# A graph layer on one core: node biases moved from bf16 products into the weights, one of four node rows normalised by ScalarE

## The chip, the cores and the metric

The kernel runs on one core of one Trainium2 chip. The metric is the device time of one execution in microseconds (us); lower is better. The engines are named as in the profile: PE is TensorE (PEld its weight loads), DVE is VectorE, ACT is ScalarE, POOL is GpSimd, SP is SyncE, which only issues transfers here. PSUM is the memory that PE writes its sums into, eight banks of 128 x 512 float32.

## The reference, cut to what matters

50,000 nodes of 256 features, 12,500 edges sorted by target `dst`.

```
h   = x @ Wn.T + bn                        # first layer: attention over the edges
a   = softmax over the edges of one dst of leaky_relu(((h[src] + edge_attr @ We.T + be) * attn).sum(-1))
x1  = layernorm(x + relu(segment_sum(h[src] * a, dst)))
                                           # second layer: dst and src change roles
mean = segment_sum(x1[dst], src) / max(count, 1)
out = layernorm(x1 + x1 @ W1.T + b1 + mean @ W2.T + b2)
```

`layernorm` takes mean and variance over the 256 features, without scale or shift. Most nodes have no edge, so for most of them `mean` is zero and `relu(...)` adds nothing.

## The kernel before

The work runs in five stages.

1. Setup: weights are loaded and turned, the edges' keys are split in digits, one-hot rows of the keys are made by DVE and ACT, and `biases` (L903 and on) writes each bias as three bf16 rows that add up to it. The identity is added into `w1T`, so that `x1 @ W1.T + x1` is one product.
2. Two counting sorts of the edges (`sort` on PE, `tiles` on DVE), by `dst` and by `src`. Beside the end of the second, POOL gathers the rows `x[src]` of 100 edge tiles, and DVE takes their dot products with the attention vector (L750 on tile `X`, `s_xdot`).
3. `by_dst`: 25 groups of four edge tiles; the first layer's aggregate is added to the nodes' rows in DRAM (`z_scratch`).
4. `dense`: 98 groups g of 512 nodes (128 partitions x 4 rows, the last one smaller). This is the stage that the change edits most.
5. `by_src`: 25 groups of edge tiles. The neighbours' mean is built, the node's own row is gathered again, both are multiplied, and the result is scattered over `out_rows`.

In `dense` each engine walks its own list in program order; only semaphores tie them together. One step of the loop, called body g here:

- PE: product of group g, first half p=0 (two rows of the four: for each row one bf16 product of `ones16` with `bias16`, L1243, then the float32 products with `w1T`, L1246); then both halves of the turn (transposes, L1236) of group g+1; then product half p=1 of group g.
- DVE: reciprocal of the deviation of x rows g+2; statistics (L915) of product half p=0 of g; normalises the four x rows of g+2 (L747); statistics of product half p=1 of g; statistics of the raw x rows g+3 (two instructions); reciprocal (L985) and `nmr` = -mean/deviation (L750) for the output of g.
- ACT: square root (L559) of the product's variance of g; square root of the x variance of g+3; then, when `nmr` is there, copies (L555) of the turned group g+2 from PSUM to `xT` and the output rows of g (L564), two at a time.

So a group's x rows are measured in one body, normalised in the next, turned in the one after it and multiplied one later. PSUM banks 0 and 1 hold turned rows, banks 4 to 7 the products, by parity of g.

In `by_src` (body q) POOL gathers own rows of q (four transfers), waits until they have landed, and scatters the output of q-3 (four transfers). PE does four aggregate tiles with a turn after each and then products with `w2T` and `w1T`, also with a bias product ahead of each row.

The functions the diff touches follow.

Of the kernel before, what the change touches and what calls it, by code (L numbers as in the profile page):

```python
# [25 lines left out]
HOOK = 48  # L26

# [25 lines left out]
def build(nc, x, src, dst, edge_attr, Wn, bn, We, be, attn, W1, b1, W2, b2, out):  # L53
# [24 lines left out]
    with ExitStack() as ctx:  # L78
# [41 lines left out]
        bias16 = sb("bias16", [P, 2, D], BF16)  # L120
# [40 lines left out]
        bias32 = agg[0][0:3, :, 0:D]  # L161
        bias_rest = agg[1][0:3, 0:2, 0:D]
# [22 lines left out]
        nmr = sb("nmr", [P, 4, GT])  # L185
        eps_c = sb("eps_c", [P, 1])

# [52 lines left out]
        s_x1 = sem("x1_ready")  # L240
# [5 lines left out]
        s_nm2 = sem("r_scales")  # L246
# [34 lines left out]
        s_enm = sem("edge_r_scales")  # L281
# [5 lines left out]
        s_rc = sems("reciprocals", 6)  # L287
# [134 lines left out]
        def _(pool):  # L422
# [90 lines left out]
            for h in range((T - sent[0]) // 2):  # L513
                pool.wait_ge(s_x1, GT * h + GT)
                order_src(2)
# [4 lines left out]
            for t in range(T):  # L520
                pool.wait_ge(s_x1, GT * (HOOK + 8 + (G - HOOK - 14) * t // T))
                wait(pool, s_nb[t % 4], 16 * (t // 4))
                gather(X[:, t, 0:D], z_dram, column(idx_dst[SRC], t), s_nb[t % 4])
# [24 lines left out]
        def _(act):  # L548
            a = nc.scalar

            def turned_copy(dst_i, src_bank, ready, n_ready, users, copied):
                act.wait_ge(ready, n_ready)
                for s, n in users:
                    wait(act, s, n)
                a.copy(xT[dst_i][:].rearrange("p a b c -> p (a b c)"), src_bank[:, :]).then_inc(copied, 1)  # L555
# [20 lines left out]
            for i, b in enumerate((bn, b1, b2)):  # L576
                act.dma_start(bias32[:, i, :], b.partition_broadcast(3)).then_inc(s_small, 16)
# [50 lines left out]
            def dense_copy(h, h_par, p):  # L628
                turned_copy(2 * h_par + p, bank[p], s_tp, 2 * h + p + 1, [(s_r, 2 * (h - 2) + p + 1)], s_tpc)
# [49 lines left out]

            root(0, s_st1, 1, s_sq1)  # L680
            root(1, s_st1, 2, s_sq1)
            for p in range(2):
                dense_copy(0, 0, p)
# [7 lines left out]
            def dense(g, m, u):  # L691
# [3 lines left out]
                act.wait_ge(s_nm2, g + 1)  # L695
# [12 lines left out]
            def by_src(q, m, u):  # L708
                def cp(p, node):
                    if in_range(q, 1, Q + 1):  # L710
                        h = q - 1
                        ready, done = (s_tc, s_tcc) if node else (s_tb[SRC], s_tbc[SRC])
                        turned_copy(2 * node + p, bank[node], ready, 2 * h + p + 1,
                                    [(s_er, 2 * (h - 1) + p + 1)], done)
# [10 lines left out]
                if in_range(q, 2, Q + 2):  # L725
                    hu = (u - 2) % 4
                    act.wait_ge(s_enm, q - 1)
# [8 lines left out]
        def _(dve):  # L736
# [166 lines left out]
            def biases():  # L903

                then(v.tensor_tensor(bias32[:, 1, :], bias32[:, 1, :], bias32[:, 2, :], ALU.add))
                rest = bias32[:, 0:2, :]
# [4 lines left out]
                v.tensor_copy(bias16[0:3], rest).then_inc(s_bias, 1)  # L911

# [19 lines left out]
            def scales(slot, rows):  # L932
                return stt(nmr[0:rows, slot, :], stats[0:rows, slot, :, 1], -1.0, rstd[0:rows, slot, :], ALU.mult, ALU.mult)

            def normalise(buf, slot, rows, ready):
                for j in range(GT):
# [25 lines left out]
            def third_stats():  # L962
                dve.wait_ge(s_x1, GT)
                first_stats(2)

            def dense(g, m, u):
# [4 lines left out]
                turns = counted(m, u, 0, 2) + 1  # L971
# [77 lines left out]
            biases()  # L1049
# [7 lines left out]

            for t in range(T):
# [57 lines left out]
            n_m = [G // 2 + (i % 2 < G % 2) for i in range(4)]  # L1116

            def by_src(q, m, u):
# [15 lines left out]
                if in_range(q, 2, Q + 2):  # L1134
                    dve.wait_ge(s_esq, q - 1)
                    invert(2 + u % 2, P, n_m[2 + u % 2] + counted(m, u, -2, 2) + 1)
                    scales(2 + u % 2, P).then_inc(s_enm, 1)
# [6 lines left out]
        def _(pe):  # L1144
# [94 lines left out]
            def products(o, terms, bias, n=P):  # L1239

                for jj in range(2):
                    to = o[0:n, jj * D:(jj + 1) * D]
                    mm(to, ones16[:, 0:n], bias16[:, bias, :], start=True, stop=False)  # L1243
                    for i, (buf, w) in enumerate(terms):
                        for c in range(2):
                            ins = mm(to, buf[:, jj, c, 0:n], w[:, c, :], start=False,  # L1246
# [4 lines left out]
            def turn(h, hu, p):  # L1251
                pe.wait_ge(s_x1, GT * h + 2 * p + 2)
# [3 lines left out]
            def product(h, par, p):  # L1256
                pe.wait_ge(s_tpc, 2 * h + p + 1)
                wait(pe, s_y, GT * (h - 2) + 2 * p + 2)
                products(rbank(par, p), [(xT[2 * par + p], w1T)], 1, parts(h)).then_inc(s_r, 1)
# [4 lines left out]

            pe.wait_ge(s_xdot, T)
# [37 lines left out]
            def by_dst(q, m, u):  # L1303
# [10 lines left out]
                def prod_b(p):  # L1314
                    if in_range(q, 1, Q + 1):
# [3 lines left out]
                        products(rbank(par, p), [(xT[2 * par + p], wnT)], 0).then_inc(s_h, 1)  # L1319
# [28 lines left out]
            def by_src(q, m, u):  # L1348
# [14 lines left out]
                if in_range(q, 1, Q + 1):  # L1363
                    h = q - 1
                    for p in range(2):
# [5 lines left out]
                        products(rbank((u - 1) % 2, p), [(xT[p], w2T), (xT[2 + p], w1T)], 1).then_inc(s_er, 1)  # L1371
# [22 lines left out]
```

## Time and profile before

| what | value |
|---|---|
| median of 3 runs | 1460.25 us (1457.04 to 1461.46) |
| profiled execution: its own time, span | 1457.04 us, 1457.1 us |
| PE busy | 1242.0 us, 85% |
| DVE busy | 1092.5 us, 75% |
| ACT busy | 784.9 us, 54% |
| POOL busy | 750.0 us, 51% |
| chain that ended last | PE 59%, DMA 9%, POOL 9%, issue 8%, ACT 7%, DVE 6% |

A busy share is an average over all five stages and says little on any one of them. In the chain of waits a stretch is put down to the engine that the end of the kernel was waiting for at that moment. PE instructions overlap: one matmul row shows a start and a duration that includes the drain, so what a matmul costs PE is the distance from one start to the next, and the chain of waits shows that distance.

### The profile page before, as it was taken

The numbers are of one execution on the slowest core, as the hardware profiler recorded it, in microseconds if no ns is written. First come the engines' busy times: TensorE is split into PE (matmuls) and PEld (weight loads), VectorE is DVE, ScalarE is ACT, GpSimd is POOL, SyncE is SP. The second block draws the span as 40 slices with busy tenths as digits, with TensorE's granted clock in tenths as the row PEclk, the third lists the DMA queues.
The fourth block names the chain that finished last, engine by engine and source line by source line (L and its number), as shares of the span: only waits on it lengthen the run. The fifth ranks groups of instructions, "written<-read, shape, count | busy, mean of one in ns | idle before, by whom it ended". The sixth has DMA issues, their size and how long they took to land.

```text
span 1457.1 us, 26741 instructions
## 1 busy us (share of the span) xinstructions
PE 1242.0 (85%) x7210; PEld 1047.6 (72%) x7210; DVE 1092.5 (75%) x3970; ACT 784.9 (54%) x1768; POOL 750.0 (51%) x731
## 2 busy tenths in 40 slices
PE   4499867960199999679999999999998999999994
PEld 3388756850088888568888888888886888778783
DVE  8888876885555555278888888888898787867761
ACT  5655773630044444347777777777764444444542
POOL 1057762677767777733433103555531555655563
PEclk9899998985599999889999999999999999999997
DMA  6889898989256666556666767898872233223221
GB/s 201 261 199 216 182 288 227 311 264 370 72 80 91 100 94 91 66 178 229 218 217 225 221 222 255 291 300 293 306 244 90 90 99 91 86 88 96 85 79 42
DMA packets 118161, 260.71 MB, mean 179 GB/s; under 512 B 23505, under 2 KB 56872, under 8 KB 118084
## 3 DMA queue, kind: packets, MB, share of 16 engines
q1 hardware_dynamic: 75738, 193.82, 42.4%
q0 software_dynamic: 40128, 64.45, 19.6%
q10 hardware_dynamic: 2218, 1.58, 0.3%
q8 instruction: 28, 0.46, 0.1%
q14 instruction: 49, 0.40, 0.1%
HBM read 182.23 MB, written 130.49 MB: 215 GB/s over the span
## 4 chain that ended last, share of the span: by engine, by line
PE 59%; DMA 9%; POOL 9%; issue 8%; ACT 7%; DVE 6%; ACTq 0%; POOLq 0%; DVEq 0%
PE bank L1246 32%; PE bank L1236 8%; PE bank L1224 5%; PE bank L1291 4%; DMA xin<-z_scratch,idx_src 4%; PE bank L1287 4%; PE bank L1243 4%; POOL out_rows L465 4%; POOL xin L462 3%; ACT aggn L602 3%; DMA X<-in_x,idx_src 2%; DVE X L747 2%; PE bank L1175 2%; DMA yout<-low_digits_scratch 2%; ACT sel L650 1%
## 5 line engine op out<-in xcount | busy, mean ns | idle before, releaser
L1246 PE MATMUL bank<-w1T,xT 128*128 128x256 f32 x1968 | 491.2, 380 | 0.0
L1246 PEld LDWEIGHTS bank<-w1T,xT 128*128 128x128 f32 x1968 | 343.4, 190 | 66.4 <-issue 0.3
L471 POOL DMA_INDIRECT order_scratch<-pay,rank_i x200 | 196.0, 980 | 240.8 <-DVE xin L747 105.9
L564 ACT ACTIVATE yout<-bank,nmr,rstd 128x256 f32<-128x256 f32 x492 | 251.7, 577 | 7.3 <-DVE nmr L750 7.3
L555 ACT COPY xT<-bank 128x512 f32<-128x512 f32 x346 | 203.0, 588 | 37.6 <-PE bank L1236 25.0
L915 DVE BATCH_NORM_STATS2 stats<-xin 128x6 f32<-128x512 f32 x246 | 158.8, 687 | 76.0 <-DMA xin<-z_scratch,idx_src 54.6
L915 DVE BATCH_NORM_STATS2 stats<-bank 128x6 f32<-128x512 f32 x246 | 168.5, 694 | 58.7 <-PE bank L1246 58.1
L663 ACT COPY agg<-bank 128x257 f32<-128x257 f32 (+1 forms) x200 | 74.4, 372 | 223.3 <-PE bank L1291 216.4
L510 POOL DMA_INDIRECT z_scratch<-xin,idx_out x100 | 156.4, 1564 | 53.3 <-ACT xin L676 30.1
L747 DVE TENSOR_SCALAR xin<-xin,stats,rstd 128x256 f32<-128x256 f32 x492 | 172.2, 412 | 1.0
L465 POOL DMA_INDIRECT out_rows<-yout,idx_out x100 | 100.0, 1000 | 140.6 <-DMA xin<-z_scratch,idx_src 71.8
L462 POOL DMA_INDIRECT X<-z_scratch,idx_dst x100 | 94.9, 949 | 141.7 <-DVE xin L747 112.5
L559 ACT ACTIVATE std<-stats,eps_c 128x4 f32<-128x4 f32 x271 | 81.0, 300 | 151.4 <-DVE stats L915 143.1
L1243 PE MATMUL bank<-bias,ones 128*128 128x256 bf16 (+1 forms) x592 | 161.5, 273 | 0.7 <-ACT yout L564 0.4
L1224 PE MATMUL bank<-sel,agg 128*128 128x196 f32 x800 | 155.8, 339 | 0.0
L1236 PE MATMUL bank<-ident,xin 128*128 128x128 f32 x984 | 132.6, 274 | 19.4 <-DVE xin L747 19.4
L1236 PEld LDWEIGHTS bank<-ident,xin 128*128 128x128 f32 x984 | 117.8, 142 | 34.8 <-issue 20.0
L1175 PE MATMUL bank<-X 128*128 128x196 bf16 x800 | 94.5, 252 | 48.6 <-ACT sel L650 23.4
L1291 PE MATMUL bank<-agg,csel 128*128 128x257 f32 (+1 forms) x396 | 122.9, 392 | 14.4 <-ACT agg L663 14.3
L1224 PEld LDWEIGHTS bank<-sel,agg 128*128 128x128 f32 x800 | 133.0, 194 | 0.5 <-DVE bank L750 0.3
L462 POOL DMA_INDIRECT X<-in_x,idx_src x100 | 99.0, 990 | 52.5 <-issue 23.4
L1287 PE MATMUL bank<-X,sel 128*128 (+2 forms) x400 | 122.6, 390 | 3.4 <-DVE csel L747 3.4
(187 smaller groups left out, 1858.5 us busy)
## 6 DMA issues: line engine op xcount, KB each, us to landing
z_scratch<-in_x SPq DMA_DIRECT2D x125, 400.0 KB
xin<-z_scratch SPq DMA_DIRECT2D x97, 512.0 KB, 4.9
out_rows<-yout SPq DMA_DIRECT2D x97, 512.0 KB, 3.1
yout<-keys_scratch SPq DMA_DIRECT2D x50, 256.0 KB, 5.0
kB<-sorted_scratch SPq DMA_DIRECT2D x50, 256.0 KB, 3.4
yout<-low_digits_scratch SPq DMA_DIRECT2D x50, 128.0 KB
xin<-in_edge_attr SPq DMA_DIRECT2D x12, 512.0 KB, 5.1
order_scratch<-pay,rank_i POOLq DMA_INDIRECT x200, 4.3
```

The costliest lines, as they stand in the source:

```text
L462: g.indirect_dma_start(out=dst_ap, out_offset=None, in_=table, in_offset=where).then_inc(s, 16)
L471: g.indirect_dma_start(out=order_dram[k], out_offset=bass.IndirectOffsetOnAxis(ap=rank_i[k][:, t:t + 1], axis=0), in_=pay[:, t, :], in_off ...
L555: a.copy(xT[dst_i][:].rearrange("p a b c -> p (a b c)"), src_bank[:, :]).then_inc(copied, 1)
L564: a.activation(yout[hu][0:rows, j, :], bank_of(j // 2)[0:rows, (j % 2) * D:(j % 2 + 1) * D], ACT.Identity, bias=nmr[0:rows, slot, j:j + 1] ...
L747: return v.tensor_scalar(o, i, s1, s2, o0, o1) if o1 is not None else v.tensor_scalar(o, i, s1, s2, o0)
L915: return v.bn_stats(stats[0:rows, slot, 2 * p:2 * p + 2, :].rearrange("p j s -> p (j s)"), pair.rearrange("p j c -> p c j"))
L1224: ins = mm(bank[3 + t % 4][:, 0:HC], onehotT[n % 2][:, b, j * P:(j + 1) * P], table[i % 2][:, b, :], start=b == 0, stop=b == 1)
L1236: ins = tr(o[:, at:at + n], buf[0:n, 2 * p + jj, c * P:(c + 1) * P], ident[0:n, 0:n])
L1243: mm(to, ones16[:, 0:n], bias16[:, bias, :], start=True, stop=False)
L1246: ins = mm(to, buf[:, jj, c, 0:n], w[:, c, :], start=False, stop=i == len(terms) - 1 and c == 1)
L1287: ins = mm(o, sel[u % 2][:, j, :], rows, start=True, stop=first)
L1291: ins = mm(o, csel[u % 2][:, j, :], before, start=False, stop=True)
```

## The change

Four edits.

- The products of `dense` and `by_src` lose their bias product. Instead `w1T` and `w2T` are centred once (`centre_weights`): the mean over the output features is taken out of every row, so that a product has mean zero over its features, and the bias is folded in as a rank-one term. ACT's copies of the turned x1 rows add 1.0 to every element; as normalised rows sum to zero over the features, x1 + 1.0 brings out exactly that term. Only `h`'s products in `by_dst` keep a bias product.
- As the products have mean zero, the output is product times 1/deviation: `nmr` is gone, and L564 becomes a `Copy` with a scale and no bias tile.
- Of the four x rows of a group in `dense`, DVE normalises three (`DROWS = 3`); the fourth is done by ACT (`act_rows`), which needs a new small tile `nmx` from DVE.
- The column sums of the centred weights are taken by four new PE products between the second sort and the attention stage.

```
-                                 ACT.Identity, bias=nmr[0:rows, slot, j:j + 1],
-                                 scale=rstd[0:rows, slot, j:j + 1]).then_inc(done, 1)
+                                 ACT.Copy, scale=rstd[0:rows, slot, j:j + 1]).then_inc(done, 1)
...
-            for i, b in enumerate((bn, b1, b2)):
-                act.dma_start(bias32[:, i, :], b.partition_broadcast(3)).then_inc(s_small, 16)
+            act.dma_start(bias32, bn.partition_broadcast(3)).then_inc(s_small, 16)
+            for i, b in enumerate((b1, b2)):
+                act.dma_start(out_bias[:, i, :], b.partition_broadcast(P)).then_inc(s_small, 16)
...
+            def act_rows(h, hu, slot, n=P):
+                act.wait_ge(s_nmx, h + 1)
+                for j in range(DROWS, GT):
+                    a.activation(xin[hu][0:n, j, :], xin[hu][0:n, j, :], ACT.Identity, bias=nmx[0:n, slot, j:j + 1],
+                                 scale=rstd[0:n, slot, j:j + 1]).then_inc(s_x1a, 1)
...
                 root(2 + u % 2, s_st2, g + 1, s_sq2, parts(g))
                 if in_range(g, 0, G - 3):
                     root((u + 1) % 2, s_st1, g + 4, s_sq1, parts(g + 3) if isinstance(g, int) else P)
-                act.wait_ge(s_nm2, g + 1)
+                if in_range(g, 0, G - 2):
+                    act_rows(g + 2, (u + 2) % 4, u % 2, parts(g + 2) if isinstance(g, int) else P)
+                act.wait_ge(s_inv2, g + 1)
...
+            def centre_weights():
+
+                then(v.tensor_tensor(shift, out_bias[:, 0, :], out_bias[:, 1, :], ALU.add))
+                dve.wait_ge(s_sums, 2)
+                then(v.tensor_tensor(shift, shift, bank[0][:, 0:D], ALU.subtract))
+                for w, sums in ((w1T, shift), (w2T, bank[0][:, D:2 * D])):
+                    sign = 1.0 / D if w is w1T else -1.0 / D
+                    for b in range(2):
+                        then(stt(w[:, b, :], sums, sign, w[:, b, :], ALU.mult, ALU.add, accum_out=spill[:, b:b + 1]))
+                    then(ts(spill[:, 2:4], spill[:, 0:2], 1.0 / D, None, ALU.mult))
+                    for b in range(2):
+                        ins = ts(w[:, b, :], w[:, b, :], spill[:, 2 + b:3 + b], None, ALU.subtract)
...
             def norm_x(g, m, u, off):
                 dve.wait_ge(s_rc[(u + off) % 2], counted(m, u, off, 2) + 1)
-                normalise(xin[(u + off) % 4], (u + off) % 2, parts(g), s_x1)
+                slot, n = (u + off) % 2, parts(g)
+                stt(nmx[0:n, slot, :], stats[0:n, slot, :, 1], -1.0, rstd[0:n, slot, :], ALU.mult, ALU.mult).then_inc(s_nmx, 1)
+                normalise(xin[(u + off) % 4], slot, n, s_x1, DROWS)
...
                 dve.wait_ge(s_sq2, g + 1)
-                v.reciprocal(rstd[0:n, slot, :], std[0:n, slot, :]).then_inc(s_rc[slot], 1)
-                dve.wait_ge(s_rc[slot], turns)
-                scales(slot, n).then_inc(s_nm2, 1)
+                v.reciprocal(rstd[0:n, slot, :], std[0:n, slot, :]).then_inc(s_inv2, 1)
...
-            def products(o, terms, bias, n=P):
+            def products(o, terms, biased=False, n=P):
...
-                    mm(to, ones16[:, 0:n], bias16[:, bias, :], start=True, stop=False)
+                    if biased:
+                        mm(to, ones16[:, 0:n], bias16[:], start=True, stop=False)
...
             def turn(h, hu, p):
-                pe.wait_ge(s_x1, GT * h + 2 * p + 2)
+                if p == 0:
+                    pe.wait_ge(s_x1, DROWS * h + 2)
+                else:
+                    pe.wait_ge(s_x1, DROWS * h + DROWS)
+                    pe.wait_ge(s_x1a, (GT - DROWS) * (h + 1))
```

On ACT, one body of `dense` ahead of the loop (`std` is a square root, `x_stats` and `r_stats` tell that the statistics of x rows or of the product are there). Before:

```order
L559 ACTIVATE std<-stats,eps_c 128x4 [waits r_stats]
L559 ACTIVATE std<-stats,eps_c 128x4 [waits x_stats]
L555 COPY xT<-bank 128x512 [waits r_ready,x1_turned,r_scales]
L564 ACTIVATE yout<-bank,nmr,rstd 128x256 x2
L555 COPY xT<-bank 128x512 [waits r_ready,x1_turned]
L564 ACTIVATE yout<-bank,nmr,rstd 128x256 x2
```

And now:

```order
L568 ACTIVATE std<-stats,eps_c 128x4 [waits r_stats]
L568 ACTIVATE std<-stats,eps_c 128x4 [waits x_stats]
L692 ACTIVATE xin<-xin,nmx,rstd 128x256 [waits x_shift_ready]
L563 ACTIVATE xT<-bank 128x512 [waits r_ready,x1_turned,r_inverse_std]
L573 ACTIVATE yout<-bank,rstd 128x256 x2
L563 ACTIVATE xT<-bank 128x512 [waits r_ready,x1_turned]
L573 ACTIVATE yout<-bank,rstd 128x256 x2
```

The row work L692 stands behind the square root that waits for `x_stats`. On PE, one body of the same stage, before:

```order
L1243 MATMUL bank<-bias,ones 128x256 [waits y_ready,x1_turned_copied]
L1246 MATMUL bank<-w1T,xT 128x256 x2
L1243 MATMUL bank<-bias,ones 128x256
L1246 MATMUL bank<-w1T,xT 128x256 x2
L1236 MATMUL bank<-ident,xin 128x128 [waits x1_turned_copied,x1_ready]
L1236 MATMUL bank<-ident,xin 128x128 x3
L1236 MATMUL bank<-ident,xin 128x128 [waits x1_turned_copied,x1_ready]
L1236 MATMUL bank<-ident,xin 128x128 x3
L1243 MATMUL bank<-bias,ones 128x256 [waits y_ready,x1_turned_copied]
L1246 MATMUL bank<-w1T,xT 128x256 x2
L1243 MATMUL bank<-bias,ones 128x256
L1246 MATMUL bank<-w1T,xT 128x256 x2
```

And now:

```order
L1277 MATMUL bank<-w1T,xT 128x256 [waits y_ready,x1_turned_copied]
L1277 MATMUL bank<-w1T,xT 128x256 x3
L1266 MATMUL bank<-ident,xin 128x128 [waits x1_turned_copied,x1_rows_by_dve]
L1266 MATMUL bank<-ident,xin 128x128 x3
L1266 MATMUL bank<-ident,xin 128x128 [waits x1_turned_copied,x1_rows_by_act,x1_rows_by_dve]
L1266 MATMUL bank<-ident,xin 128x128 x3
L1277 MATMUL bank<-w1T,xT 128x256 [waits y_ready,x1_turned_copied]
L1277 MATMUL bank<-w1T,xT 128x256 x3
```

The L1243 rows are gone, and the second turn waits for ACT's row (`x1_rows_by_act`) as well. On DVE, one body now:

```order
L983 RECIPROCAL rstd<-std 128x4 [waits x_std]
L949 BN_STATS stats<-bank 128x6 [waits r_ready]
L769 SCALAR_TENSOR_TENSOR nmx<-stats,rstd 128x4 [waits reciprocals1]
L766 TENSOR_SCALAR xin<-xin,stats,rstd 128x256 x3
L949 BN_STATS stats<-bank 128x6 [waits r_ready]
L949 BN_STATS stats<-xin 128x6 [waits x_loaded0]
L949 BN_STATS stats<-xin 128x6
L1017 RECIPROCAL rstd<-std 128x4 [waits r_std]
```

The order of the statistics is as before: those of the raw x rows stand behind those of the product's second half.

## Rows read from the trace of the kernel before

**Rows 1.** Busy time of each engine in dense and in the middle of by_src.

```profile
core 0: us, PE busy (x) PEld busy (x) DVE busy (x) ACT busy (x) POOL busy (x), PEclk, DMA share, GB/s
628.90:1097.90 469.00, 468.57 (x2746) 394.24 (x2744) 415.34 (x1084) 340.57 (x779) 186.27 (x197) 1.00 0.74 246
1151.00:1376.00 225.00, 216.89 (x1152) 183.53 (x1151) 171.93 (x539) 105.95 (x253) 130.21 (x133) 0.99 0.30 92
```

**Rows 2.** Chain of waits over one body of dense: start us, us, what.

```profile
801.06 0.87 PE bank L1246 x4
...
803.88 0.87 PE bank L1236 x8
804.75 0.11 PE bank L1243
...
805.83 0.86 PE bank L1246 x4
```

**Rows 3.** Timeline of that body, DVE and ACT: start us, us, engine, line, names.

```profile
801.96 0.70 DVE L915 BATCH_NORM_STATS2 stats<-bank 128x6 f32<-128x512 f32 x1 [0.41 <-PE bank L1246]
...
802.58 1.29 DVE L915 BATCH_NORM_STATS2 stats<-xin 128x6 f32<-128x512 f32 x2
802.70 0.30 ACT L559 ACTIVATE std<-stats,eps_c 128x4 f32<-128x4 f32 x1 [0.21 <-DVE stats L915]
...
803.90 0.30 ACT L559 ACTIVATE std<-stats,eps_c 128x4 f32<-128x4 f32 x1 [0.91 <-DVE stats L915]
...
804.48 0.18 DVE L952 RECIPROCAL rstd<-std 128x4 f32<-128x4 f32 x1 [0.34 <-ACT std L559]
...
805.20 1.36 DVE L747 TENSOR_SCALAR xin<-xin,stats,rstd 128x256 f32<-128x256 f32 x4
```

**Rows 4.** ACT's groups by form, whole kernel: busy us, mean ns.

```profile
L564 ACT ACTIVATE yout<-bank,nmr,rstd 128x256 f32<-128x256 f32 x488 | 249.7, 577 | 6.9 <-DVE nmr L750 6.9
...
L663 ACT COPY agg<-bank 128x257 f32<-128x257 f32 x100 | 37.5, 375 | 86.4 <-PE bank L1291 82.0 <-PE bank L1287 4.4
...
L602 ACT ACTIVATE aggn<-yout,slot_f 128x512 bf16<-128x512 bf16 x50 | 36.1, 722 | 62.7 <-PE bank L1224 43.0 <-DMA yout<-low_digits_scratch 19.7
```

**Rows 5.** Timeline, three square roots behind each other.

```profile
1095.17 0.70 ACT L559 ACTIVATE std<-stats,eps_c 128x4 f32<-128x4 f32 x3
```

**Rows 6.** Timeline, a PE that stood still and the copies that release it.

```profile
1427.20 1.07 ACT L555 COPY xT<-bank 128x512 f32<-128x512 f32 x2 [5.37 <-PE bank L1236]
...
1427.93 0.63 PE L1236 MATMUL bank<-ident,aggn 128*128 128x128 f32 x4 [0.33 <-ACT xT L555]
```

**Rows 7.** Chain of waits, products of two groups near the start of by_src.

```profile
1116.24 1.73 PE bank L1246 x8
...
1128.83 1.73 PE bank L1246 x8
```

**Rows 8.** Chain of waits, middle of by_src.

```profile
1217.47 0.99 POOL xin L462
...
1221.29 3.48 DMA xin<-z_scratch,idx_src
...
1230.88 0.99 POOL xin L462
```

**Rows 9.** Timeline, DVE in setup.

```profile
40.70 0.41 DVE L908 CAST bias<-agg 3x512 bf16<-3x512 f32 x1
...
62.15 0.29 DVE L750 SCALAR_TENSOR_TENSOR xin<-xin,u_b 128x128 f32<-128x128 f32 x1 [1.05 <-DMA xin<-in_edge_attr]
```

**Rows 10.** Timeline, DVE's first wait in the dot products.

```profile
338.03 0.46 DVE L750 SCALAR_TENSOR_TENSOR xT<-X,v_b 128x256 f32<-128x256 f32 x1 [0.43 <-DMA X<-in_x,idx_src]
```

**Rows 11.** Timeline, PE's next work behind them.

```profile
385.26 0.45 PE L1266 MATMUL bank<-ident,xdot 128*100 128x128 f32 x1 [68.96 <-DVE xT L750]
```

**Rows 12.** Timeline, DVE at the last group's output.

```profile
1438.31 0.16 DVE L750 SCALAR_TENSOR_TENSOR nmr<-stats,rstd 128x4 f32<-128x4 f32 x1
```

**Rows 13.** Timeline, PE at the start of dense.

```profile
627.20 1.94 PE L1236 MATMUL bank<-ident,xin 128*128 128x128 f32 x8 [19.43 <-DVE xin L747]
```

**Rows 14.** Busy time and granted clock of that stretch, columns as in rows 1.

```profile
626.00:629.00 3.00, 1.80 (x9) 1.60 (x10) 2.93 (x11) 0.89 (x2) 1.02 (x1) 0.50 0.44 178
```

More of the change, by code:

```diff
@@ L26 @@
 HOOK = 48
+DROWS = 3
 def wait(eng, sem, value):
@@ L184, in build @@
         rstd = sb("rstd", [P, 6, GT])
-        nmr = sb("nmr", [P, 4, GT])
         eps_c = sb("eps_c", [P, 1])
+        nmx = sb("nmx", [P, 2, GT])
         s_w = sem("weights_loaded")
@@ L286, in build @@
         s_ysc = sems("y_scattered", 4)
-        s_rc = sems("reciprocals", 6)
+        s_rc = {slot: sem(f"reciprocals{slot}") for slot in (0, 1, 4, 5)}
         s_den = sems("denominators", 2)
@@ L554, in turned_copy @@
                     wait(act, s, n)
-                a.copy(xT[dst_i][:].rearrange("p a b c -> p (a b c)"), src_bank[:, :]).then_inc(copied, 1)
+                a.activation(xT[dst_i][:].rearrange("p a b c -> p (a b c)"), src_bank[:, :], ACT.Copy,
+                             bias=raised).then_inc(copied, 1)
             def root(slot, ready, n, done, rows=P):
@@ L678, in _ @@
             steps(act, Q + 1, 4, 8, 2, by_dst)
+            def act_rows(h, hu, slot, n=P):
[3 more added lines that the diff above has]
+                                 scale=rstd[0:n, slot, j:j + 1]).then_inc(s_x1a, 1)
             root(0, s_st1, 1, s_sq1)
             root(1, s_st1, 2, s_sq1)
+            for h in range(2):
+                act_rows(h, h, h)
             for p in range(2):
@@ L901, in ordered_ends, with h_bias @@
                     v.tensor_tensor(idx_out[k][:], trash[:], keyc[k][:, 0:T], ALU.add).then_inc(s_idx, 1)
-            def biases():
-                then(v.tensor_tensor(bias32[:, 1, :], bias32[:, 1, :], bias32[:, 2, :], ALU.add))
-                rest = bias32[:, 0:2, :]
+            def h_bias():
+                rest = bias32
                 for i in range(2):
@@ L930, in invert, with normalise @@
                 dve.wait_ge(s_rc[slot], h)
[L932 to L936, printed above, removed]
+            def normalise(buf, slot, rows, ready, n=GT):
+                for j in range(n):
                     ts(buf[0:rows, j, :], buf[0:rows, j, :], stats[0:rows, slot, j, 1:2], rstd[0:rows, slot, j:j + 1],
@@ L1048, in _ @@
                 v.tensor_tensor(w1T[:, b, b * P:(b + 1) * P], w1T[:, b, b * P:(b + 1) * P], ident[:], ALU.add)
-            biases()
+            h_bias()
             features()
@@ L1056, in _ @@
                         ORDER_AT + 2: (lambda: ordered_ends(DST),)})
+            centre_weights()
             for t in range(T):
@@ L1115, in _ @@
             steps(dve, G, 4, 4, 6, dense, (HOOK, HOOK + 8))
-            n_m = [G // 2 + (i % 2 < G % 2) for i in range(4)]
+            n_m = [G // 2 + (i % 2 < G % 2) for i in range(2)]
             def by_src(q, m, u):
@@ L1135, in by_src @@
                     dve.wait_ge(s_esq, q - 1)
-                    invert(2 + u % 2, P, n_m[2 + u % 2] + counted(m, u, -2, 2) + 1)
-                    scales(2 + u % 2, P).then_inc(s_enm, 1)
+                    v.reciprocal(rstd[:, 2 + u % 2, :], std[:, 2 + u % 2, :]).then_inc(s_einv, 1)
                 if in_range(q, 0, Q):
@@ L1237, in turn_pair @@
                 return ins
[L1239 removed]
+            def products(o, terms, biased=False, n=P):
                 for jj in range(2):
                     to = o[0:n, jj * D:(jj + 1) * D]
[L1243 removed]
+                    if biased:
+                        mm(to, ones16[:, 0:n], bias16[:], start=True, stop=False)
                     for i, (buf, w) in enumerate(terms):
                         for c in range(2):
[L1246 removed]
+                            ins = mm(to, buf[:, jj, c, 0:n], w[:, c, :], start=not biased and i == 0 and c == 0,
                                      stop=i == len(terms) - 1 and c == 1)
@@ L1263, in _ @@
             sort(SRC, {ORDER_AT: lambda: turn_ordered(DST), ORDER_AT + 1: lambda: shift_ordered(DST)})
+            pe.wait_ge(s_bias, 1)
+            for i, w in enumerate((w1T, w2T)):
+                for b in range(2):
+                    ins = mm(bank[0][:, i * D:(i + 1) * D], ones[:], w[:, b, :], start=b == 0, stop=b == 1)
+                ins.then_inc(s_sums, 1)
+            pe.wait_ge(s_centred, 1)
             pe.wait_ge(s_xdot, T)
```

43 lines of the change are left out of this document (26 added, 17 removed).

## The prediction, made before the result was known

> **What bounds the kernel now.** I read the profile in this order: the busy time by stretch, the chain of waits in each stage, then the timeline of one body where the chain names PE. In `dense` PE is busy 468.6 of 469.0 us, DVE 415.3, ACT 340.6, at full granted clock [rows 1]: PE has no gap. The chain gives the shares of a body: 0.11 for a bias product, 0.87 for the four float32 instructions of a row, 0.87 for the eight transposes, and from 801.06 to 805.83 a period of 4.77 us [rows 2]. That is 4 x (0.11 + 0.87) + 0.87 = 4.79. The stage's 98 bodies are 469 us, a third of the kernel. In the middle of `by_src` PE is busy 216.9 of 225 us, but the chain runs through POOL and the transfers: four gathers issued from 1217.47, the last one's landing (3.48 us), the scatters, and the next gathers at 1230.88 [rows 8], 13.4 us a group. Near its start the chain names PE alone, 12.59 us a group from 1116.24 to 1128.83 [rows 7]; its end is alike.
>
> **The change, part by part, in `dense`.** PE loses four bias products a body, 4 x 0.11 = 0.44, so its own work falls to 4.33. DVE loses one row of four (1.36 / 4 = 0.34) [rows 3] and `nmr` (0.16) [rows 12] and gains `nmx` of the same size: 415.3 / 98 - 0.34 = 3.9 of work a body. ACT gains one row: 340.6 / 98 + 0.6 = 4.1 [rows 1]. If only work counted, every engine would fit into 4.33.
>
> But the row on ACT ties a knot. Follow what PE's second turn of group g+2 now waits for. It stands in PE's body g+1, ahead of that body's product half p=1. It needs ACT's row of g+2. On ACT that row stands in body g behind the square root of x rows g+3 (the order on ACT in the section on the change). That root waits for DVE's statistics of x rows g+3, and these stand on DVE behind the statistics of product half p=1 of g, which PE has just ended. So from the end of one product half p=1 to the end of the next, no part can run ahead:
>
> - PE's last matmul of g to DVE: 801.06 + 0.87 = 801.93 to 801.96, 0.03 [rows 2, 3]
> - product statistics: 801.96 to 802.58, 0.62 [rows 3]
> - statistics of x rows g+3, two instructions: 1.29, ending at 803.87 [rows 3]
> - to ACT's root: 803.87 to 803.90, 0.03 [rows 3]
> - root until the next ACT instruction may start: three roots in 0.70, each 0.30, so 0.20 apart [rows 5]
> - ACT's row: 0.58, see below
> - ACT's end to PE's first transpose: of two copies in 1.07, each 0.59, the first ends at 1427.79; PE starts at 1427.93: 0.14 [rows 6]
> - four transposes of a PE that stood still: 0.63 [rows 6] (in full flow 0.43 [rows 2])
> - product half p=1, two rows of 0.87 without bias: 1.73 [rows 2, 7]
>
> The sum is 5.25 us, above both the 4.33 of PE's work and the 4.77 of now. Before, this ring did not exist: DVE normalised all four rows of g+2 between the two halves' statistics of g, well ahead, and ACT's root of g+3 fed only DVE's next reciprocal. The cover that hid ACT's 0.91 wait for the x statistics [rows 3] is gone: the row now queues behind it, and PE, which had no gap, waits about 0.9 us a body.
>
> The row itself is not in the trace. Nearest above it: `yout` with the same scale and bias tiles and the same 256 elements, but from PSUM, 577 ns; below: a plain copy of 257 elements, 375 ns; farther above: 512 bf16 elements from SBUF with one tile operand, 722 ns [rows 4]. I take 577 as 0.58, having the same operands. The 0.14 could be 0.03, as from DVE to ACT, or 0.28, as from ACT's root, ended at 804.20, to DVE's reciprocal at 804.48 [rows 3], where a loop's registers are read in between, as ahead of PE's second turn. So the ring is between 5.25 - 0.20 - 0.11 = 4.94 and 5.25 + 0.14 + 0.14 = 5.53.
>
> Bodies 0 to 94 have x rows g+3 to measure, so 95 bodies pay 5.25 - 4.77 = +0.48: +45.6 us. The last three save the bias: 3 x 0.44 = -1.3. What ACT does after the row (two copies and four outputs: 3.5 a body less two roots of 0.3, 2.9) ends at 2.17 + 0.58 + 2.9 = 5.65 after a product's end, ahead of the next product's root at 5.25 + 0.68 = 5.93: no second ring. That `yout` loses an operand changes nothing, for ACT has room; nor does the copy's added 1.0.
>
> **Outside `dense`.**
> - `by_src`: four bias products a group, 0.44. In the 17 or so groups that POOL and the transfers bind [rows 8] this gives nothing. In some seven, at the start and at the end, PE binds: up to 7 x 0.44 = 3.1. I take -2.5; floor 0.
> - Setup: the bias rows are half as wide and one addition goes. Two casts of 0.41 and two 0.74 steps halve, and a cast and an addition of about 0.4 shrink or go [rows 9]: 1.5 us on DVE, but behind it DVE waits 1.05 for edge features at 62.15 [rows 9], so part of it goes into that wait. I take -1, between 0 and -1.5. The biases now go to all 128 partitions; two small transfers more at a time when DVE has other work: 0.
> - `centre_weights`: some 13 DVE instructions of 0.4 to 0.6 with a wait behind each, and four PE products, 6 to 8 us. They stand ahead of the dot products. There DVE runs behind until 338.03 and from then on waits for the gathers, until PE gets its turn at 385.26 [rows 10, 11]. A dot product takes 0.35 back to back and a gather 1.25, so a lag of 8 us is made good some 11 us later, long before 385. Cost 0; if the cover were gone, +8.
> - The last output: `nmr` (0.16 and its wait) goes: -0.3 [rows 12].
>
> Sum: 45.6 - 1.3 - 2.5 - 1.0 - 0.3 = +40.5 on the profiled execution's 1457.1, 1497.6. The median of the three runs lies 3.2 above that execution, so 1501 compared with 1460.25.
>
> **Rivals.**
> - A: the ring does not bind, PE stays the bound without its bias products. 98 x -0.44 = -43.1, with the other terms -3.8: -47, 1413. For it: every engine's work fits. Against: the ring is built of starts and ends in rows 2 to 6, and each link is fixed by program order. It would need the ring at 4.33, that is 0.9 shorter; the row at its lower bound and the fastest relay give 0.3. Chance 7%.
> - B: near no change. The row at 0.37, the relay 0.03 and transposes that run at 0.43 though PE waited: 5.25 - 0.21 - 0.11 - 0.20 = 4.73, so 95 x -0.04 and -5: 1452. Every link would have to be at its best. Chance 4%, and 4% for the space between A and this.
> - C: the clock. PE now pauses in every body. Half clock is in the trace at the start of `dense`: eight transposes in 1.94 at a granted 0.50 [rows 13, 14], where in full flow they take 0.87 a turn [rows 2]. PE's part of the ring would double, +2.3 a body, some +220 us: 1720. Against it: in the middle of `by_src` PE loses 8 us in pieces and the clock stays at 0.99 [rows 1]. Chance 3%. The Trainium skill's "TensorE: Matmul & The Clock Gate", section "A second HAM failure mode: psum-queue depth-cycling", tells of a kernel whose PE paused between groups and whose clock went to and fro; no run here shows that yet.
> - D: the ring holds and a link that I set at nothing adds to it (the sequencer's waits on registers, DVE's port shared with ACT's write): above 5.53, over 1530. Chance 6%.
>
> **How the numbers follow.** The forecast, the ring between 4.94 and 5.53, has 76%: 1501, its own range 1470 to 1530. A has 7, B and the space beside it 8, C 3, D 6. The range for 8 of 10 is 1473 to 1525, mostly the inner part of the forecast's own. What three runs can tell from no change is 0.3%, 4.4 us. Faster: A, B and part of the low end, 12%; within 0.3%: 3%; slower: the rest, 85%.
>
> **What would show it.** If I am right, PE's busy share in `dense` falls from 100% to about 83%; the second turn of each body shows a wait of 0.8 to 0.9 us released by ACT's new row; that row follows the root for x statistics by 0.2; the period is 5.2 and repeats. The 0.41 that DVE waited ahead of the product statistics grows to about 1. The time before 620 hardly moves, and `by_src` ends 2 to 3 us sooner for its start. If PE has no gap and the period is 4.33, rival A holds and the ring was misread. If the clock in `dense` is well below 1, it is C. A row of 0.4 instead of 0.58 would put the result near 1481.

## The result and the profile after

| | median us | runs |
|---|---|---|
| before | 1460.66 | 1457.04 to 1461.46 (4) |
| after | 1505.43 | 1503.14 to 1506.37 (4) |

The ratio is 1.0308, with a 95% interval from 1.0294 to 1.0323: slower by 45 us. The forecast was 1501 (1473 to 1525).

PE's busy time fell from 1242.0 to 1212.3 us, DVE's from 1092.5 to 1043.9, ACT's from 784.9 to 777.6, and the kernel became slower all the same. The stages, each from its first PE product to that of the next (the span's end for the last):

| stage | before | after |
|---|---|---|
| up to `dense`'s first product | 629.2 | 630.1 |
| `dense` | 469.7 | 515.2 |
| `by_src` | 358.3 | 359.0 |

Here are the same stretches of the changed kernel that [rows 1] gives for the kernel before, `dense` whole and the middle of `by_src` (columns: stretch, its length, busy us and instructions of PE, PEld, DVE, ACT, POOL; granted clock, DMA share, GB/s):

```profile
630.10:1145.30 515.20, 446.28 (x2354) 378.29 (x2353) 373.17 (x989) 341.13 (x874) 184.99 (x195) 1.00 0.68 224
1190.00:1440.00 250.00, 231.40 (x1193) 199.16 (x1191) 182.37 (x570) 108.74 (x275) 145.70 (x145) 0.99 0.29 89
```

PE is busy 87% of `dense` instead of all of it, at full clock (the matmul records include the drain, so the pauses are longer than the rest of 13%: 5.27 less 4.33 is 18%). The timeline of one body of the changed kernel, PE, DVE and ACT (in brackets: idle time before the row and what ended it):

```profile
805.06 0.70 DVE L949 BATCH_NORM_STATS2 stats<-bank 128x6 f32<-128x512 f32 x1 [1.17 <-PE bank L1277]
...
805.67 1.29 DVE L949 BATCH_NORM_STATS2 stats<-xin 128x6 f32<-128x512 f32 x2
...
807.00 0.30 ACT L568 ACTIVATE std<-stats,eps_c 128x4 f32<-128x4 f32 x1 [0.91 <-DVE stats L949]
807.20 0.58 ACT L692 ACTIVATE xin<-xin,nmx,rstd 128x256 f32<-128x256 f32 x1
...
807.91 0.65 PE L1266 MATMUL bank<-ident,xin 128*128 128x128 f32 x4 [0.73 <-ACT xin L692]
...
808.40 3.62 PE L1277 MATMUL bank<-w1T,xT 128*128 128x256 f32 x16
...
810.33 0.70 DVE L949 BATCH_NORM_STATS2 stats<-bank 128x6 f32<-128x512 f32 x1 [1.17 <-PE bank L1277]
```

Read downwards it is the ring of the prediction: statistics of the product at 805.06, of the x rows at 805.67, ACT's root at 807.00, its row at 807.20, PE's second turn at 807.91 after 0.73 of waiting for that row, the product, and at 810.33 the next statistics. The period is 5.27 us. In the chain of waits of the changed kernel (start, us, what) PE has two pieces in each period, and DVE, ACT and short stretches of "issue" have the rest, where before it was PE alone [rows 2]:

```profile
807.91 0.65 PE bank L1266 x4
808.57 1.74 PE bank L1277 x8
...
810.95 0.50 DVE stats L949
811.45 0.10 issue
811.55 0.69 DVE stats L949
...
812.47 0.59 ACT xin L692
813.07 0.12 issue
813.19 0.65 PE bank L1266 x4
```

### The profile page after: what moved, and what is told of

Same layout as the page of the kernel before. It is cut to its first block, busy times and chain, and to the rows that moved or that the text cites. A ratio compares the mean times of both kernels' runs of the same rounds, so it can differ in the third digit from the quotient of the medians.

```text
span 1504.3 us, 25842 instructions
## 1 busy us (share of the span) xinstructions
PE 1212.3 (81%) x6726; PEld 1030.4 (68%) x6726; DVE 1043.9 (69%) x3862; ACT 777.6 (52%) x1866; POOL 749.9 (50%) x731
## 4 chain that ended last, share of the span: by engine, by line
PE 41%; DVE 14%; issue 14%; POOL 11%; ACT 9%; DMA 9%; ACTq 1%; DVEq 0%; POOLq 0%; SPq 0%
PE bank L1277 20%; DVE stats L949 8%; PE bank L1266 7%; DMA xin<-z_scratch,idx_src 5%; POOL out_rows L473 5%; PE bank L1254 5%; POOL xin L470 4%; PE bank L1333 3%; PE bank L1329 3%; ACT aggn L611 3%; ACT xin L692 3%; DVE X L766 2%; PE bank L1205 2%; DMA yout<-low_digits_scratch 2%; DMA X<-in_x,idx_src 2%
## 5 line engine op out<-in xcount | busy, mean ns | idle before, releaser
L1277 PE MATMUL bank<-w1T,xT 128*128 128x256 f32 x1968 | 459.6, 381 | 0.0
L1277 PEld LDWEIGHTS bank<-w1T,xT 128*128 128x128 f32 x1968 | 367.2, 191 | 46.2 <-ACT xT L563 0.2
L1266 PE MATMUL bank<-ident,xin 128*128 128x128 f32 x984 | 153.0, 279 | 88.0 <-ACT xin L692 58.3
L563 ACT ACTIVATE xT<-bank 128x512 f32<-128x512 f32 x346 | 204.3, 592 | 17.4 <-PE bank L1266 10.0
L573 ACT ACTIVATE yout<-bank,rstd 128x256 f32<-128x256 f32 x492 | 203.1, 477 | 5.6 <-DVE rstd L1167 5.2
L766 DVE TENSOR_SCALAR xin<-xin,stats,rstd 128x256 f32<-128x256 f32 x394 | 139.9, 412 | 0.9
L470 POOL DMA_INDIRECT xin<-z_scratch,idx_src x100 | 99.7, 997 | 55.5 <-issue 30.4
```

Of the source, the lines that this page charges most:

```text
L470: g.indirect_dma_start(out=dst_ap, out_offset=None, in_=table, in_offset=where).then_inc(s, 16)
L563: a.activation(xT[dst_i][:].rearrange("p a b c -> p (a b c)"), src_bank[:, :], ACT.Copy, bias=raised).then_inc(copied, 1)
L766: return v.tensor_scalar(o, i, s1, s2, o0, o1) if o1 is not None else v.tensor_scalar(o, i, s1, s2, o0)
L1266: ins = tr(o[:, at:at + n], buf[0:n, 2 * p + jj, c * P:(c + 1) * P], ident[0:n, 0:n])
L1277: ins = mm(to, buf[:, jj, c, 0:n], w[:, c, :], start=not biased and i == 0 and c == 0, stop=i == len(terms) - 1 and c == 1)
```

## The experiments

Times are medians in us; the ratio is to the kernel before, run on the same chip.

| run | median | ratio, 95% interval | `dense` | `by_src` |
|---|---|---|---|---|
| row ahead of the roots | 1422.18 | 0.9743, 0.9727 to 0.9759 | 427.6 | 361.3 |
| four rows on DVE | 1422.58 | 0.9749, 0.9733 to 0.9766 | 427.4 | 360.0 |
| two rows on ACT | 1548.77 | 1.0614, 1.0596 to 1.0632 | 556.9 | 357.4 |
| before, row on ACT | 1525.47 | 1.0454, 1.0436 to 1.0471 | 536.0 | 351.6 |
| before, no bias in `by_src` | 1458.81 | 0.9994, 0.9982 to 1.0007 | 470.5 | 356.1 |
| row ahead, bias loads late | 1417.21 | 0.9723, 0.9700 to 0.9745 | 427.3 | 359.9 |
| row ahead, no landing wait | 1391.24 | 0.9533, 0.9510 to 0.9557 | 426.8 | 334.4 |
| x statistics earlier | 1429.81 | 0.9808, 0.9781 to 0.9836 | 438.2 | 359.3 |
| before, no landing wait | 1447.27 | 0.9910, 0.9881 to 0.9939 | 470.8 | 345.7 |
| all three | 1390.79 | 0.9521, 0.9491 to 0.9551 | 427.8 | 334.4 |

### The row moved ahead of the roots

```
             def dense(g, m, u):
+                if in_range(g, 0, G - 2):
+                    act_rows(g + 2, (u + 2) % 4, u % 2, parts(g + 2) if isinstance(g, int) else P)
                 root(2 + u % 2, s_st2, g + 1, s_sq2, parts(g))
                 if in_range(g, 0, G - 3):
                     root((u + 1) % 2, s_st1, g + 4, s_sq1, parts(g + 3) if isinstance(g, int) else P)
-                if in_range(g, 0, G - 2):
-                    act_rows(g + 2, (u + 2) % 4, u % 2, parts(g + 2) if isinstance(g, int) else P)
```

Expected:

> The changed kernel with ACT's row of g+2 moved ahead of both square roots of the body. Ring theory: the row no longer waits for the statistics of x rows g+3, the ring is cut and PE's own work of 4.33 us sets the body instead of 5.27: 98 x 0.94 = 92 less than 1505, 1413. Rival 'load' (ACT has too much to do in a body, wherever the row stands): no change, 1505. Rival 'products' (the products without bias product or the centred weights are what is slower): 1505.

Measured: 1422.18, 83 us below the changed kernel. The same instructions, in another order on one engine. The timeline:

```profile
802.79 0.63 ACT L692 ACTIVATE xin<-xin,nmx,rstd 128x256 f32<-128x256 f32 x1
803.10 1.28 DVE L949 BATCH_NORM_STATS2 stats<-xin 128x6 f32<-128x512 f32 x2
803.28 0.33 ACT L568 ACTIVATE std<-stats,eps_c 128x4 f32<-128x4 f32 x1
...
804.01 1.04 PE L1266 MATMUL bank<-ident,xin 128*128 128x128 f32 x8
```

and the chain of waits, PE alone again, with 4.33 us from product to product (3.46 + 0.87):

```profile
804.17 0.87 PE bank L1266 x8
805.04 3.46 PE bank L1277 x16
808.50 0.55 PE bank L1266 x5
```

The row starts 1.2 us before the transposes and ends 0.6 before them; PE has no gap. Both rivals, load and products, fall: ACT has exactly the load it had. The result is 9 above the 1413 expected. `dense` gained 87.6, not 92: I had taken 98 bodies instead of the 95 that are in the ring, 2.8 us; the other 1.6 I can't place. The rest lies outside: in this run `dense` starts 1.6 later and `by_src` is 2.3 longer than in the changed kernel, both within the spread of these stages from trace to trace (see "What was off").

### All four rows on DVE

```
-DROWS = 3
+DROWS = 4
...
-                act.wait_ge(s_nmx, h + 1)
...
-                stt(nmx[0:n, slot, :], stats[0:n, slot, :, 1], -1.0, rstd[0:n, slot, :], ALU.mult, ALU.mult).then_inc(s_nmx, 1)
...
-                    pe.wait_ge(s_x1a, (GT - DROWS) * (h + 1))
```

Expected:

> The changed kernel, but DVE normalises all four x rows; no row on ACT, no nmx. Ring theory: no ring, 4.33 us a body by PE, DVE's work is 4.1: 1413 to 1418. Load theory: the same 1413 to 1418. Products theory: 1505. With the run of the row moved ahead this tells what the row on ACT is worth to DVE once it hangs in no ring: by the ring theory nothing, since PE binds.

Measured: 1422.58, the same as with the row on ACT ahead of the roots; `dense` 427.4 against 427.6. Relieving DVE by a row is worth nothing at a body of 4.33: DVE was busy 363.3 of 390 us in a stretch of this run, and 344.9 with the row on ACT, and PE 390.0 in both. So the change's gain in `dense`, 469.7 to 427.4, is PE's: 42.3 us, 0.43 for each of 98 bodies, the four bias products at 0.11. Its loss comes from the row where it stands.

### Two rows on ACT

```
-DROWS = 3
+DROWS = 2
```

Expected:

> The changed kernel with two of four x rows on ACT instead of one. Ring theory: the ring holds the second row as well, which starts 0.46 after the first: 5.27 + 0.46 = 5.73 us a body, 95 x 0.46 = +44, 1549. Load theory: ACT has 3.5 of work in 5.27 and takes the second row into its idle time: 1505 to 1510.

Measured: 1548.77, 43 above the changed kernel. One body:

```profile
806.86 0.70 DVE L949 BATCH_NORM_STATS2 stats<-bank 128x6 f32<-128x512 f32 x1 [1.91 <-PE bank L1277]
...
809.00 1.08 ACT L692 ACTIVATE xin<-xin,nmx,rstd 128x256 f32<-128x256 f32 x2
...
810.13 0.66 PE L1266 MATMUL bank<-ident,xin 128*128 128x128 f32 x4 [1.15 <-ACT xin L692]
...
812.55 0.70 DVE L949 BATCH_NORM_STATS2 stats<-bank 128x6 f32<-128x512 f32 x1 [1.92 <-PE bank L1277]
```

The second row passes into the ring nearly whole: 5.69 a body against 5.27 with one row, 0.42 more, where the two rows together take 0.50 longer than one (1.08 and 0.58). ACT's idle time doesn't take it in. The load theory expected 1505 to 1510.

### The kernel before with ACT's row alone

Here `nmx`, `act_rows` and PE's two waits are put into the kernel before as the change has them; bias products, `nmr` and weights stay.

```
+                if in_range(g, 0, G - 2):
+                    act_rows(g + 2, (u + 2) % 4, u % 2, parts(g + 2) if isinstance(g, int) else P)
                 act.wait_ge(s_nm2, g + 1)
...
-                pe.wait_ge(s_x1, GT * h + 2 * p + 2)
+                if p == 0:
+                    pe.wait_ge(s_x1, DROWS * h + 2)
+                else:
+                    pe.wait_ge(s_x1, DROWS * h + DROWS)
+                    pe.wait_ge(s_x1a, (GT - DROWS) * (h + 1))
```

Expected:

> The kernel before with one edit alone: the fourth x row on ACT, behind both roots; bias products, nmr and weights as they were. Ring theory: the ring holds two bias products more, 5.27 + 0.22 = 5.49 us a body against 4.77: 95 x 0.72 = +68, 1529. Products theory: the row is harmless, 1461. If it comes out at 1529, removing the bias products alone took 0.22 a body out of the ring, and the row put 0.72 in.

Measured: 1525.47. The body is as expected, from one product's statistics to the next 5.49:

```profile
807.91 0.70 DVE L929 BATCH_NORM_STATS2 stats<-bank 128x6 f32<-128x512 f32 x1 [1.39 <-PE bank L1262]
...
813.40 0.70 DVE L929 BATCH_NORM_STATS2 stats<-bank 128x6 f32<-128x512 f32 x1 [1.15 <-PE bank L1262]
```

`dense` is 536.0, 66.3 more than before, where 68 were expected; in this run `by_src` was 6.7 shorter than before although nothing in it was changed (below). So the row costs 66 us with the bias products and 87.8 without them (515.2 against 427.4). Leaving them out takes four bias products from a body that PE alone bounds (4.77 to 4.33), but only two from the ring (5.49 to 5.27), since the other two lie outside it: the distance between the two grows.

### Statistics of the x rows earlier

```
                     if p == 0 and more2:
                         norm_x(g + 2, m, u, 2)
+                    if p == 0 and more3:
+                        stats_x(g + 3, m, u, 3, 0)
+                        stats_x(g + 3, m, u, 3, 1)
                 ins.then_inc(s_st2, 1)
-                if more3:
-                    stats_x(g + 3, m, u, 3, 0)
-                    stats_x(g + 3, m, u, 3, 1)
```

Expected:

> The changed kernel with ACT's row where the change put it, behind both roots; instead DVE takes the statistics of x rows g+3 ahead of those of the second product half. Ring theory: 1.29 us of statistics leave the ring; DVE comes to the second half's statistics up to 0.4 late instead, the ring is at most 4.5 a body and PE's own 4.33 the floor: 1422 to 1440. Rival (a row behind the roots on ACT costs by itself, since it delays the outputs): 1500 to 1505.

Measured: 1429.81, with ACT's row where the change put it. The timeline shows the two roots now directly behind each other and the row at once behind them:

```profile
802.19 1.30 DVE L949 BATCH_NORM_STATS2 stats<-xin 128x6 f32<-128x512 f32 x2
...
803.41 0.68 DVE L949 BATCH_NORM_STATS2 stats<-bank 128x6 f32<-128x512 f32 x1
804.12 0.49 ACT L568 ACTIVATE std<-stats,eps_c 128x4 f32<-128x4 f32 x2 [0.52 <-DVE stats L949]
...
804.52 0.59 ACT L692 ACTIVATE xin<-xin,nmx,rstd 128x256 f32<-128x256 f32 x1
```

This cuts another link of the same ring than the first experiment, and 75.6 us go, so standing behind the roots is not by itself what costs 88 us. It isn't free either: `dense` takes 438.2, 4.47 a body (4.5 at most was expected), 10.6 us more than with the row ahead of the roots. DVE now comes to the second half's statistics 0.1 to 0.3 late, and between 790 and 830 us of the trace the bodies take 4.33 and 4.52 in turn: in every other one PE's second turn stands until ACT's row is done, and the eight transposes take 1.05 instead of 0.87.

### `by_src` without its bias product

```
-                        products(rbank((u - 1) % 2, p), [(xT[p], w2T), (xT[2 + p], w1T)], 1).then_inc(s_er, 1)
+                        products(rbank((u - 1) % 2, p), [(xT[p], w2T), (xT[2 + p], w1T)], 1, biased=False).then_inc(s_er, 1)
```

Expected:

> The kernel before with one edit: by_src's products without their bias product (b1 + b2 is missing in the rows scattered there). The prediction's theory: some seven groups of by_src are bound by PE and give back 0.44 each, -2.5 to -3: 1457. Rival: with PE relieved, the loop of POOL and its gathers takes those groups over at once, and by_src, which took 359.0 us in the changed kernel against 358.3 before, gives nothing: 1459 to 1461.

Measured: 0.9994 with an interval from 0.9982 to 1.0007, -0.9 us and anything from -2.6 to +1.0. It doesn't tell 0 from the -2.5 that the prediction took. Its trace has `by_src` at 356.1, 2.2 shorter; but the stage varies by more than that from run to run: 358.3 before and 351.6 with ACT's row in the kernel before, with the same code in the stage.

### The scatters without the wait for the gathers

```
                 if q >= 3:
                     h = q - 3
                     pool.wait_ge(s_ey, GT * h + GT)
-                    if q < Q:
-                        pool.wait_ge(s_xs[q % 4], 16 * GT * (q // 4 + 1))
```

Expected:

> The kernel with the row moved ahead, and POOL in by_src no longer waits for its four gathers to land before it issues four scatters (they read other tiles than the gathers write, and other rows in DRAM). Theory that the POOL loop sets by_src: the landing of 3.5 to 3.8 us leaves the loop, POOL has 10.4 a group, PE's 12.15 binds: 20 x (13.8 - 12.2) = -32, 1390. Rival: the gathers' landing is on DVE's and PE's path too (the rows must be measured and turned), or it gets longer with scatters beside it: 1415 to 1425.

Measured: 1391.24, 31 below the run with the row moved ahead (expected -32). The stage itself gives 26.9 of them, 361.3 to 334.4; most of the rest is that `dense` starts at 628.5 in this trace and at 631.7 in the other, with the same code ahead of it. In `by_src` PE is now busy all the time, and the chain of waits is PE alone, 12.15 us a group from 1183.34 to 1195.49:

```profile
1110.00:1340.00 230.00, 230.00 (x1215) 202.02 (x1214) 188.92 (x586) 111.22 (x284) 150.00 (x153) 1.00 0.33 100
```

```profile
1183.34 6.91 PE bank L1275 x32
...
1195.49 6.91 PE bank L1275 x32
```

POOL now waits for the outputs only (the rows show the last of four gathers and the first of four scatters):

```profile
1195.39 0.95 POOL L470 DMA_INDIRECT xin<-z_scratch,idx_src  x1 [0.31 <-issue]
1198.41 1.06 POOL L473 DMA_INDIRECT out_rows<-yout,idx_out  x1 [2.08 <-ACT yout L571]
```

The first scatter starts 3.0 us after the last gather's issue. With the wait it started 0.89 us after that gather's landing, that is 3.6 to 5.1 us after its issue. Here, of the five groups of this stretch whose landings are in the trace, the last gather took 2.7 to 2.9 us in four and 4.6 in one. So it had mostly just landed when the scatters began, and the run hardly tests scatters beside gathers in flight.

### The kernel before without that wait

The same two lines taken out of the kernel before. Expected:

> The kernel before with one edit: POOL's scatters in by_src don't wait for the gathers to land. Theory (the POOL loop hid the bias products of by_src): PE's 12.6 a group with bias products binds now, 13.6 before in 17 groups: 17 x -1.0 = -17, 1443. Together with the run of the row moved ahead, without the landing wait, whose groups took 12.15, this says that the bias products of by_src are worth 0.44 x 25 = 11 us once the loop is gone. Rival (the loop was not it, the gain came from elsewhere): 1459.

Measured: 1447.27, against 1459.87 in the same runs, -12.6; 1443 were expected. The trace's `by_src` is 345.7, 12.6 shorter, and PE-bound at 12.59 a group, in the chain of waits from 1233.69 to 1246.28:

```profile
1233.69 1.73 PE bank L1244 x8
...
1246.28 1.73 PE bank L1244 x8
```

With centred weights the same stage is 334.4: the bias products of `by_src` are worth 11.3 us, 25 x 0.44 = 11.0 expected, but only once POOL's loop is gone. With the loop in place, leaving them out gave -0.9, anything from -2.6 to +1.0.

### The bias loads issued late, and all three together

```
-            for i, b in enumerate((b1, b2)):
-                act.dma_start(out_bias[:, i, :], b.partition_broadcast(P)).then_inc(s_small, 16)
...
                 act.dma_start(lowrow_dram[k], lowrow[k]).then_inc(s_keyd[k], 16)
+            for i, b in enumerate((b1, b2)):
+                act.dma_start(out_bias[:, i, :], b.partition_broadcast(P)).then_inc(s_outb, 16)
...
-            dve.wait_ge(s_small, 96)
+            dve.wait_ge(s_small, 64)
...
             def centre_weights():
+                dve.wait_ge(s_outb, 32)
```

Expected:

> The kernel with the row moved ahead, and the two bias loads to all 128 partitions issued behind the key rows' stores and on a semaphore of their own, so that DVE's first steps don't wait for them. Theory: the 1.10 us that DVE waited for them in the changed kernel goes, and up to that much is seen before the gathers' stage; behind it the gathers bind, so the end moves by 0 to -1: 1421 to 1422. Rival: the late start was passed on to the end: 1420 to 1421. The two may be too close to tell; the trace tells whether DVE's one-hot rows start at 11.4 instead of 12.5 and when the dot products end.

> The changed kernel with the row moved ahead, the bias loads late and no landing wait: 1391 less what the late bias loads give, 0 to 3 us: 1388 to 1391. If the late loads only freed time that the gathers' stage hides, 1391.

In the changed kernel DVE waits for these loads at the very start:

```profile
11.79 0.48 DVE L801 TENSOR_SCALAR attn_b<-ones,attn_c 128x128 f32<-128x128 f32 x2 [1.10 <-DMA out_bias<-in_L_gnn_b]
```

With late loads the one-hot rows start at 11.31 instead of 12.47:

```profile
11.31 1.87 DVE L767 TENSOR_SCALAR X<-iota,dig_f 128x256 bf16<-128x256 bf16 x10
```

Measured: 1417.21 against 1422.18 for the same kernel with early loads, but the two were run on different occasions and their intervals of the ratio overlap; and with the landing wait gone 1390.79 against 1391.24. The wait of 1.1 us is shown to go. That it reaches the end is not shown, and most of the 5.0 can't be its doing: `dense` starts at 628.2 with late loads and at 631.7 with early ones, 3.5 apart, but at 628.7 and 628.5 in the pair without the landing wait. 1390.79 is the fastest version, equal to the one without late loads.

## Why the prediction was right

**The ring.** It was worked out link by link, and nearly every link came out as written (the forecast in brackets). From PE's end to the statistics 0.02 (0.03), to those of the x rows 0.61 (0.62), these 1.29 (1.29), to ACT's root 0.04 (0.03), root to row 0.20 (0.20), ACT's end to PE's transposes 0.13 (0.14), these 0.65 (0.63), product 1.74 (1.73). The sum was 5.25 and the period is 5.27; ahead of the loop and behind it, where waits stand on constants and not on registers, the bodies took 5.22. The row itself came to 585 ns:

```profile
L692 ACT ACTIVATE xin<-xin,nmx,rstd 128x256 f32<-128x256 f32 x97 | 56.7, 585 | 0.7 <-DVE nmx L769 0.7
```

I had taken 0.58 from `yout`'s 577 [rows 4]; the 0.585 worked out from the Trainium skill's "ScalarE: Activation LUTs", section "What ACT_TABLE_LOAD costs", was exact here. As source SBUF and PSUM are 8 ns apart in these rows (585 for this row, 577 for `yout`). The figure isn't a constant: with the row ahead of the roots the same instruction took 632. `dense` was forecast at +44.3 (45.6 for the ring, -1.3 for the last bodies) and measured at +45.5. Of the signs named, PE's wait ahead of the second turn was 0.73 (0.8 to 0.9), DVE's ahead of the product statistics 1.17 (about 1), and PE's busy share 87% (83%, which is 4.33 of 5.27; the records count the drain as busy).

**That it is this ring.** Cut on ACT (row ahead): 87.6 us go. Cut on DVE (x statistics earlier): 77.0 go. Lengthened by a second row: +41.7, where 0.46 for 95 bodies would be 43.7. Put into the kernel before: +66.3. And without a row on ACT the stage is PE's 4.33. A load is ruled out by the first experiment, and the links leave nothing over for a port shared by ACT and DVE: they add up to the period, and the statistics of the x rows took 1.29 in the ring and before. Rival D is out, as is C, with the clock at 1.00 in `dense`. Rival A, 1413, was the right account of `dense` without the row's place; its terms outside `dense` didn't come, and the time was 1422.

**What was off, by size.** Between the two profiled executions the change cost 47.2 us where 40.5 were forecast: 1.2 in `dense`, the rest in the terms outside it, which were to give 3.8 and lost 1.7. The medians differ by 44.8, so the sum came nearer than its terms. The terms outside `dense` are also smaller than what one trace can tell: in four traces with the code of the kernel before ahead of `dense`, its first product lies between 628.1 and 632.0, and `by_src` with the landing wait takes between 351.6 and 361.3 over all traces.
- `by_src`: -2.5 forecast, +0.7 measured. The step "in some seven groups PE binds: up to 3.1" took the whole of PE's share as a gain, but the POOL loop stands right behind PE. The chain holds 21 landings of gathers, in the kernel before 17, and the run without the bias products of `by_src` also 21. In that run's last groups, where PE had bound before, the loop takes 12.62 and 12.73 us (gathers issued at 1385.47, 1398.09, 1410.82, landing in 2.7 to 2.8), and PE had needed 12.63 and 12.70 there: there is next to nothing to gain. As a time this can't be told from the forecast (-0.9, from -2.6 to +1.0).
- Setup: -1 forecast, 1.0 later measured at the first product of `dense` (630.1, 629.2), within the spread just given. The bias steps did shrink, though not by half (0.41 to 0.28 and 0.74 to 0.47), and the features start at 43.31 instead of 43.63; but the two loads that I set at 0 cost DVE 1.10 at the start. PE's turn behind the gathers comes at 385.35, before at 385.26 [rows 11]; in the four traces just named it comes between 383.8 and 388.1, so neither the -1 nor the +1.0 can be read from one trace of each.
- `centre_weights`: 5.7 us (316.31 to 321.97), 6 to 8 forecast. The cover is in the trace: DVE comes to its first wait for a gather at 344.92 instead of 338.03 [rows 10] and then still waits 25.5 us for gathers in all before 385.
- The last output: from the reciprocal's start to `yout` 0.21, before 0.41 (1438.10 to 1438.51) (the 0.16 of `nmr` [rows 12] and its wait are gone), and four `yout` rows took 1.57, before 1.93: 0.6 instead of 0.3.
- The step from the profiled execution to the median: in every later run the span is some 1.8 below the run's own time (1504.3 and 1506.16 here), so the span of 1457.1 before belongs to a time of about 1459, not to the 1457.04 that stands in the table ahead of the prediction. The 3.2 added is 1.8 of that kind and 1.3 to the median, and holds as a sum.

**What stays open.** Why `by_src` is 351.6 in one trace and 358.3 in another, both with bias products and the landing wait. On the chain, the landing of the last gather has a median of 2.96 us in the first and of 3.67 in the second, and the loop of POOL carries that difference 15 to 20 times; what makes it land late was not tried. Nor is it known why, without the landing wait, it mostly lands in 2.7 to 2.9. That loop hides every small gain of PE there.

## What to carry to other kernels

Giving work to an engine with idle time needs two questions beyond its load: what stands ahead of it in that engine's order, and whether what it waits for hangs, over the other engines, on the consumer's own last result. Here 0.58 us of work a body, on an engine that is busy two thirds of the stage, cost 88 us, since it stood behind a wait for statistics that follow the product before; the same instruction two places up cost nothing. When such a ring appears, add up its links from starts and ends in the timeline: the sum is the period, and it can be cut at any link. And work taken from the engine that bounds a stage gives little when another bound stands close behind it: leaving the same bias products out of `by_src` gave -0.9 us, from -2.6 to +1.0, with the landing wait, and 11.3 us without it.

## What the runs showed of the hardware

- An output row of ACT with one tile operand less (scale from a tile, no bias tile) took 477 ns instead of 577. The Trainium skill's "ScalarE: Activation LUTs", section "What ACT_TABLE_LOAD costs", gives about 93 ns for each such operand; these rows agree, with 100.
- A gap of 0.7 us in every body of 5.27 us left PE at its full 2.4 GHz: the granted clock was 1.00 over `dense` in the changed kernel. With two rows on ACT the gap was 1.15 in 5.69, and the clock 1.00 as well.
- In `by_src`, POOL's first scatter started 0.89 us after the landing that it waited for; with gathers that land in 2.7 to 2.8 us the loop of four gathers, landing and four scatters took 12.6 to 12.7 us. Without the wait the groups went from 13.8 us on average to the 12.15 that PE sets, and a scatter's issue stayed at 1.0 us.
- The ring took 5.27 us in the loop and 5.22 outside it. That the 0.05 are the waits whose value comes from a loop's registers is inferred, not tested.
